# Two groups of spectral columns per turn in the middle stage of a Fourier MLP kernel, one 64-row stretch per turn, and the shared tile's relu on ScalarE

## The chip, the cores and the metric

The kernel runs on one core of a Trainium2 chip. The metric is the device time of one execution, in microseconds; lower is better. All data is fp32.

## The reference

An image batch `x` of shape (4, 128, 128, 768) goes through a Fourier layer: a real 2-D FFT over the two spatial axes, two small complex matrix layers in every spectral point, and the inverse FFT. The 768 channels fall into 8 blocks of 96, and each block has its own weights.

```
xf = rfft2(x, axes=(1, 2), norm='ortho')            # 65 columns kw, 128 rows kh
o1r = relu(xr @ w1[0] - xi @ w1[1] + b1[0]);  o1i = relu(xi @ w1[0] + xr @ w1[1] + b1[1])
o2r = o1r @ w2[0] - o1i @ w2[1] + b2[0];      o2i = o1i @ w2[0] + o1r @ w2[1] + b2[1]
o   = softshrink(o2, 0.01)                          # sign(v) * max(|v| - 0.01, 0)
out = irfft2(o, norm='ortho') + x
```

## The kernel before

The work is cut into 32 units (4 images times 8 channel blocks of 96). Each unit passes through six stages on TensorE: A (transform along one axis), B (first layer, on columns that are not yet transformed along the other axis; the two commute), C (transform along the other axis), D (second layer), E and F (inverse transforms). The next unit's stage A is mixed in after the present unit's inverse. An fp32 product appears in the trace as two MATMUL records, so a group's count is twice that of the code.

This case is about the middle of a unit, stages B, C and D, which the kernel calls `layers`. The 65 spectral columns are cut into `GROUPS`, 17 steps `s`: most have four columns (eight real and imaginary parts), step `REAL` = 2 holds columns 0 and 64, and the last has three. One step consists of:

- B whole, `stage_b_whole` (L778): four products with 128 contracted rows; B halved, `stage_b_halved` (L790): four products with 64 contracted rows, two row halves of the array at a time. A complex column needs 192 rows of input, so 128 + 64. VectorE then copies the result from PSUM to `mixed` (L655), and counts `b_copied`.
- C, `stage_c` (L807): six products with 128 rows, out of `mixed` into three tiles, of which the middle one is shared by the two halves. Their relu goes to `hidden` on ScalarE (L530, L533, `relu_done`), and the shared tile's relu to `middle` on VectorE (L668, `middle_done`).
- D outer, `stage_d_outer` (L822): four products with 128 rows; D middle, `stage_d_middle` (L832): four with 64 rows. They add to a bias that VectorE wrote to PSUM before (L678, the "seed"). ScalarE then computes the `excess` (L524), and VectorE the shrunk result (L663, `shrunk`), back into the spectrum.

ScalarE also gathers the columns of the next step into `whole` (L493, L494) and `halved` (L495, L496). `whole`, `halved`, `mixed`, `hidden` and `middle` have two buffers each, `excess` has one.

Every engine runs its own list in the order in which the code is written, and waits on semaphores. In turn `s` TensorE does B whole of step s, D of step s-2 (outer, middle), B halved of s, C of s-1. So each turn has one stretch of 64-row products (D middle, then B halved), and C works on a step whose copy to `mixed` was made one turn ago. Turns 0 and 1 have no D, and the last two steps' D have stretches of their own: 19 stretches in a unit. PSUM has eight banks: B takes 0 and 1 (step 1: 6 and 7), C takes 2 and 3, D takes 4 and 5 or 6 and 7, by the step's parity. `flip` (L839, L840), four records of 192 moving elements, symmetrises the `REAL` step's result.

Of the kernel before, what the change touches and what calls it, by code (L numbers as in the profile page):

```python
# [27 lines left out]
REAL = 2  # L28

# [130 lines left out]
def fourier_mlp(nc, x, w1, b1, w2, b2, dft, out):  # L160
    with ExitStack() as ctx:
# [26 lines left out]
        excess = sb("excess", [SIZE, BLOCK, 8])  # L188
        real_kw = sb("real_kw", [SIZE, BLOCK, 6])
# [32 lines left out]
        def banks_b(s):  # L222

            return 6 if s == 1 else 0

        def bank_b(s, k):

            if s == 1:
                return bank_d(s)[:, 2 * k:2 * k + 2]
            return bank(banks_b(s) + k // 2)[:, (k % 2) * 2 * BLOCK:(k % 2 + 1) * 2 * BLOCK]  # L230

        def both_b(s, i=None):
            if s == 1:

                return psum[:, banks_b(s):banks_b(s) + 2, 4 * i * SIZE // 2:4 * (i + 1) * SIZE // 2].rearrange(
                    "p y (r n) -> p y r n", r=2)[:, :, :, 0:BLOCK]
            return psum[:, banks_b(s):banks_b(s) + 2, 0:4 * BLOCK].rearrange("p y (i o) -> p i y o", i=2)


        bank_c = bank(2).rearrange("p (y i h) -> p y i h", y=2, i=2)  # L240
        middle_c = bank(3, SIZE, 2 * SIZE).rearrange("p (i h) -> p i h", i=2)

        def bank_d(s):

            pair = psum[:, 4 + 2 * (s % 2):6 + 2 * (s % 2), :].rearrange("p y n -> p (y n)")
            return pair.rearrange("p (q n) -> p q n", q=8)[:, :, 0:BLOCK]

# [7 lines left out]
        bank_flip = bank(0, SIZE, 2 * BLOCK).rearrange("p (k c) -> p k c", k=2)  # L255
# [36 lines left out]
        a_done, act_copied, dve_copied = sem("a_done"), sem("act_copied"), sem("dve_copied")  # L292
        b_done, b_copied = sem("b_done"), sem("b_copied")
# [90 lines left out]
        def _(sp):  # L384
# [10 lines left out]
            sp.dma_start(excess[:, :, :].rearrange("p a b -> p (a b)")[:, 0:2 * SIZE],  # L395
# [73 lines left out]
        def _(act):  # L469
            def gather(s):  # L470
                w, h, first = whole[s % 2], halved[s % 2], GROUPS[s][0]
                if s == REAL:
# [3 lines left out]
                    act.activation(h[0:HALF, :, 0], im[0:HALF, 0], ACT.Copy)  # L476
                    act.activation(h[HALF:SIZE, :, 0], im[0:HALF, 1], ACT.Copy).then_inc(halved_gathered, 1)
                    return
                j = 2 + 2 * first
                if s == 0:  # L480

                    act.activation(w[0:BLOCK, :, slice(*INNER)], first_parts(*INNER)[0:BLOCK, 0], ACT.Copy).then_inc(whole_gathered, 1)  # L482
                    return
                if GROUPS[s][3] is None:
# [3 lines left out]
                    act.activation(w[BLOCK:SIZE, 1, :, 0], U[HALF:BLOCK, :, j + 5], ACT.Copy).then_inc(whole_gathered, 1)  # L488
                    act.activation(h[0:HALF], U[0:HALF, :, j + 2:j + 4], ACT.Copy)
                    act.activation(h[HALF:SIZE, :, 0], U[0:HALF, :, j + 5], ACT.Copy).then_inc(halved_gathered, 1)  # L490
                    return
                parts = U[:, :, j:j + 8].rearrange("p s (y c r) -> p c y s r", y=2, c=2)
                act.activation(w[0:BLOCK], parts[0:BLOCK, 0], ACT.Copy)  # L493
                act.activation(w[BLOCK:SIZE], parts[HALF:BLOCK, 1], ACT.Copy).then_inc(whole_gathered, 1)  # L494
                act.activation(h[0:HALF], parts[0:HALF, 1, 0], ACT.Copy)  # L495
                act.activation(h[HALF:SIZE], parts[0:HALF, 1, 1], ACT.Copy).then_inc(halved_gathered, 1)  # L496

            def forward(n):
                for at in A_ACT:
                    act.wait_ge(a_done, n * NA + (at + 1))  # L500
                    src = bank_a(at).rearrange("p (s j) -> p s j", s=A_ROWS)
                    rows, third = evict_views(A_ORDER[at])
                    act.activation(rows, src[0:BLOCK], ACT.Copy)
                    act.activation(third, src[BLOCK:], ACT.Copy).then_inc(act_copied, 1)
            def layers(m, par, n):
# [4 lines left out]
                gather(0)  # L510
                act.wait_ge(w_loaded[par], (m + 1) * W_LOADS * 16)
                for s in range(NS + 2):
                    if s + 1 < NS:
                        if s >= 1:
                            act.wait_ge(b_done, n * NS + s)
                        gather(s + 1)

                    for stage in ("sums", "tiles") if s < NS else ("tiles", "sums"):
                        if stage == "sums" and s >= 2:
                            t = s - 2  # L520
                            act.wait_ge(d_done, n * NS + (t + 1))
                            if t >= 1:
                                act.wait_ge(shrunk, n * NS + t)
                            act.activation(excess[:, :, 0:rows_d(t)], parts_d(t), ACT.Relu,  # L524
                                           bias=over[:, 0:1]).then_inc(excess_done, 1)
                        if stage == "tiles" and 1 <= s <= NS:
                            t = s - 1
                            act.wait_ge(c_done, n * NS + (t + 1))
                            tiles = hidden[t % 2]
                            act.activation(tiles[:, 0, 0:pairs(t)], bank_c[:, 0, 0:pairs(t)], ACT.Relu,  # L530
                                           bias=b1t[par][:, 0:1]).then_inc(relu_done, 1)
                            k = pairs(t) if None not in GROUPS[t] else 1
                            act.activation(tiles[:, 1, 0:k], bank_c[:, 1, 0:k], ACT.Relu,  # L533
                                           bias=b1t[par][:, 2:3]).then_inc(relu_done, 1)
                act.wait_ge(flip_done, n + 1)
                act.activation(U[:, 0:BLOCK, SIZE + 2:].rearrange("p c k -> p k c"), bank_flip,
                               ACT.Copy).then_inc(flip_copied, 1)
            def inverse(n):
# [23 lines left out]
        def _(dve):  # L562
            dve.memset(over[:, :], -LAMBDA).then_inc(padding_set, 1)
            iw = excess[:, :, :].rearrange("p a b -> p (a b)")[:, 0:2 * SIZE].rearrange("p (a b) -> p a b", a=2)
# [52 lines left out]
            def forward(n):  # L617
# [26 lines left out]
                dve.tensor_copy(halved[0][HALF:SIZE, slice(*INNER)], parts[0:HALF, 1, 1]).then_inc(first_halved, 1)  # L644
            def layers(m, par, n, first, last):
                for s in range(NS + 2):
                    if s < NS:
                        k = pairs(s)
                        dve.wait_ge(b_done, n * NS + (s + 1))
                        if s == 1:  # L650
                            for i in range(2):
                                flat = mixed[s % 2][:, i].rearrange("p y (r o) -> p y r o", r=2)
# [277 lines left out]
```

## Time and profile before

| | |
|---|---|
| time, median of 3 runs | 5098.28 us (5097.17 to 5102.1) |
| span of the profiled execution | 5094.2 us |
| TensorE matmul busy | 4981.3 us, 98% |
| TensorE weight load busy | 4673.3 us, 92% |
| VectorE busy | 3816.7 us, 75% |
| ScalarE busy | 2996.3 us, 59% |
| GpSimd busy | 1436.3 us, 28% |
| mean granted TensorE clock | 0.993 |

The span runs from the first to the last instruction of one profiled execution. A matmul's record lasts longer than the time until the next one can start, since they are pipelined, so the busy share of TensorE says that it hardly ever stands still, and not that it works at its peak. What a stage costs is seen in the distances between the starts of its groups.

### The profile page before, as it was taken

Reading aid. Unit: us, or ns where it says so; the run is one execution under the profiler, and the core shown is the slowest. Engines: PE = TensorE matmul, PEld = TensorE weight load, DVE = VectorE, ACT = ScalarE, POOL = GpSimd, SP = SyncE. Lnnn points to the kernel's source line nnn. Section 1 sums busy time; section 2 is a strip of 40 time slices with the busy share of each in tenths; the row PEclk is TensorE's granted clock in tenths of the full one; section 3 lists DMA queues with packets and bytes.
Section 4 is the critical chain, followed back from the end, with each engine's and each line's share of the span. In section 5 each row is a group of like instructions: output and inputs, shape, how many; then the busy total and the mean of one; then the engine's idle time right before and its main releaser. Section 6 shows DMA issues by size and latency. Waiting matters only on the chain.

```text
span 5094.2 us, 113221 instructions
## 1 busy us (share of the span) xinstructions
PE 4981.3 (98%) x40000; PEld 4673.3 (92%) x40000; DVE 3816.7 (75%) x6159; ACT 2996.3 (59%) x5409; POOL 1436.3 (28%) x905
## 2 busy tenths in 40 slices
PE   6999999999999999999999999999999999999997
PEld 6999999999999999999999999999999999999996
DVE  5777777777777777777777777777777777777876
ACT  4555655556655566555566555665556655556653
POOL 3033223332123332233321333312333123332220
PEclk8999999999999999999999999999999999999998
DMA  5044423444323443234442344432344323444233
GB/s 114 12 94 105 98 59 69 91 105 105 68 57 87 105 105 87 56 81 94 105 105 52 70 90 105 106 70 62 79 105 106 86 61 78 92 105 105 61 73 72
DMA packets 1699712, 430.24 MB, mean 84 GB/s; under 512 B 1698848, under 2 KB 1698976, under 8 KB 1699104
## 3 DMA queue, kind: packets, MB, share of 16 engines
q1 hardware_dynamic: 1696768, 421.83, 37.5%
q8 instruction: 346, 5.67, 0.5%
q14 instruction: 262, 2.15, 0.1%
q10 hardware_dynamic: 2336, 0.59, 0.1%
HBM read 220.84 MB, written 201.33 MB: 83 GB/s over the span
## 4 chain that ended last, share of the span: by engine, by line
PE 96%; DVE 2%; issue 1%; SPq 1%; ACT 0%; DMA 0%; DVEq 0%; ACTq 0%
PE psum L807 15%; PE psum L778 14%; PE psum L822 14%; PE psum L760 13%; PE psum L849 13%; PE psum L832 9%; PE psum L790 7%; PE psum L859 3%; PE psum L860 3%; PE psum L861 3%; DVE mixed L655 1%; SPq L387 1%; DVE spectrum L628 0%; PE psum L840 0%; PE psum L839 0%
## 5 line engine op out<-in xcount | busy, mean ns | idle before, releaser
L655 DVE COPY mixed<-psum 128x768 f32<-128x768 f32 (+1 forms) x512 | 477.4, 932 | 700.0 <-PE psum L790 700.0
L541 ACT ACTIVATE sums_high<-psum 128x512 fp32r<-128x512 f32 x768 | 459.2, 599 | 731.3 <-PE psum L849 731.2
L807 PEld LDWEIGHTS psum<-mats,mixed 128*128 128x128 f32 x6272 | 744.0, 191 | 121.2 <-issue 113.1
L807 PE MATMUL psum<-mats,mixed 128*128 128x128 f32 x6272 | 841.8, 283 | 0.0
L778 PE MATMUL psum<-w_whole,whole 128*128 128x192 f32 x4160 | 782.3, 330 | 40.9 <-ACT whole L482 11.4
L822 PE MATMUL psum<-w2t,hidden 128*128 128x192 f32 x4160 | 771.7, 328 | 0.0
L849 PE MATMUL psum<-mats,spectrum 128*128 128x128 f32 x6144 | 743.7, 275 | 3.1 <-DVE spectrum L663 1.6
L760 PE MATMUL psum<-mats,x 128*128 128x128 f32 x6144 | 704.9, 277 | 33.6 <-DVE x L582 17.8
L760 PEld LDWEIGHTS psum<-mats,x 128*128 128x128 f32 x6144 | 696.0, 193 | 40.9 <-issue 23.0
L778 PEld LDWEIGHTS psum<-w_whole,whole 128*128 128x128 f32 x4160 | 673.3, 197 | 60.6 <-issue 33.7
L849 PEld LDWEIGHTS psum<-mats,spectrum 128*128 128x128 f32 x6144 | 714.5, 192 | 4.1 <-DVE sums_low L701 2.0
L701 DVE TENSOR_TENSOR sums_low<-psum,sums_high 128x512 fp32r<-128x512 f32 x768 | 530.4, 691 | 248.8 <-ACT sums_high L541 248.7
L822 PEld LDWEIGHTS psum<-w2t,hidden 128*128 128x128 f32 x4160 | 685.9, 190 | 13.4 <-issue 7.2
L524 ACT ACTIVATE excess<-psum,over 128x768 f32<-128x768 f32 (+1 forms) x544 | 481.8, 886 | 332.8 <-PE psum L832 329.9
L530 ACT ACTIVATE hidden<-psum,b1t 128x256 f32<-128x256 f32 (+1 forms) x544 | 254.6, 468 | 688.8 <-PE psum L807 688.8
L453 POOL TENSOR_TENSOR x<-x,half 128x3072 f32<-128x3072 f32 x32 | 169.8, 5307 | 1450.0 <-DVE halved L644 1450.0
L663 DVE SCALAR_TENSOR_TENSOR spectrum<-psum,excess 128x768 f32<-128x768 f32 (+1 forms) x512 | 480.8, 939 | 118.7 <-ACT excess L524 113.0
L678 DVE COPY psum<-b_rows 128x768 f32<-128x768 f32 (+1 forms) x544 | 504.0, 926 | 0.0
L436 POOL TENSOR_TENSOR x<-x 128x192 f32<-128x192 f32 x31 | 15.7, 505 | 1700.4 <-DMA x<-x 1700.4
L832 PE MATMUL psum<-w2t,middle 64*128 64x192 f32 x4160 | 490.3, 350 | 0.0
L859 PE MATMUL psum<-sums_high,iw_high 128*128 128x260 f32 (+1 forms) x1536 | 461.8, 301 | 0.0
L445 POOL TENSOR_TENSOR x<-x,doubled 128x640 f32<-128x640 f32 (+1 forms) x248 | 443.4, 1788 | 17.0
(76 smaller groups left out, 7800.7 us busy)
## 6 DMA issues: line engine op xcount, KB each, us to landing
x<-x SPq DMA_DIRECT2D x736, 192.0 KB, 2.9
out<-x SPq DMA_DIRECT2D x736, 192.0 KB, 2.5
x<-x SPq DMA_DIRECT2D x736, 64.0 KB, 2.6
out<-x SPq DMA_DIRECT2D x736, 64.0 KB, 2.2
x<-x SPq DMA_DIRECT2D x32, 144.0 KB, 2.7
out<-x SPq DMA_DIRECT2D x32, 144.0 KB, 2.3
w2t<-L_conv_w SPq DMA_DIRECT2D x124, 36.0 KB, 1.8
x<-x SPq DMA_DIRECT2D x64, 48.0 KB, 2.4
```

What stands on the lines that cost most here:

```text
L524: act.activation(excess[:, :, 0:rows_d(t)], parts_d(t), ACT.Relu, bias=over[:, 0:1]).then_inc(excess_done, 1)
L655: copied = dve.tensor_copy(mixed[s % 2][:, 0:k], both_b(s)[:, 0:k])
L663: dve.scalar_tensor_tensor(dst, parts_d(t), LAMBDA, excess[:, :, 0:rows], op0=ALU.add, op1=ALU.min).then_inc(shrunk, 1)
L678: dve.tensor_copy(bank_d(s).rearrange("p (k r) c -> p k r c", r=2)[:, 0:k], b2_rows[par][:, :, :].unsqueeze(1).broadcast_to([SIZE, k, 2, B ...
L701: dve.tensor_tensor(sums_low[:, q % RING], bank_e(q), sums_high[:, q % RING], ALU.subtract).then_inc(low_copied, 1)
L760: last = pe.matmul(bank_a(at)[:, i * SIZE:(i + 1) * SIZE], xs[par][:, j, :], mat(FW_EVEN if g[0] < NP else FW_ODD), start=i == 0, stop=Tru ...
L778: pe.matmul(bank_b(s, k), whole[s % 2][:, k // 2, :, k % 2], w1_whole[par][:, :, :].rearrange("p r o -> p (r o)"), start=k % 2 == 0, stop= ...
L807: last = pe.matmul(out[tile], flat[:, tile * SIZE:(tile + 1) * SIZE], mat(FH), start=True, stop=True)
L822: pe.matmul(sums_d(s, k), hidden[s % 2][:, k // 2, k % 2], w2_tile(par, slice(0, SIZE), 2 * (k // 2)), start=False, stop=False, skip_group ...
L832: last = pe.matmul(sums_d(s, i + 2 * y), middle[s % 2][rows, i], w2_tile(par, rows, 1), start=False, stop=True, skip_group_check=True)
L849: last = pe.matmul(bank_e(q)[:, :, i], U[:, q * CHUNK + i, 4:], mat(IH_FIRST if q * CHUNK < THIRD else IH), start=True, stop=True)
L859: pe.matmul(out, iw_high[:, j], high, start=True, stop=False)
```

## The change

`layers` takes two steps a turn (`STEPS`: nine turns, the last with one step). With a and b the two steps of a turn and p and q those of the turn before, TensorE does: B whole a, B whole b, D outer p, D outer q, D middle p, D middle q, B halved a, B halved b, C a, C b. The 64-row stretch holds the second layer's tiles first and the first layer's last. In the first turn each step has its own B whole and B halved. After the ninth turn come `flip` and D of step 16.

With it:

- B and C of one step share a pair of banks (`pair_bc`: 0 and 1 for even steps, 6 and 7 for odd ones), D takes 4 and 5 or 2 and 3. B whole of step s therefore waits for the relus of step s-2.
- C of a step follows in the same turn as its B halved.
- ScalarE takes over the relu of the shared tile (`rectify`: three ACTIVATE instead of two), and `excess` has two buffers. ScalarE's order in a turn: gather whole for both steps ahead, gather halved for the first of them, the excess of p and q, the relus of a and b, gather halved for the second step ahead.
- VectorE's order in a turn: copy a, copy b, shrink p, shrink q, seed a, seed b, then what belongs to neighbouring units.
- The `REAL` step's result is stored part by part (`real_kw` is [6, 96] a partition, and was [96, 6]), so `flip` reads runs of 96 adjacent elements where it read every sixth by distance.
- In stage A the row `MIDDLE` is transformed first in its group; some start flags of A and F differ. TensorE waits for step 15's shrink before the next unit's stage A.

The diff, cut to its core (`MIDDLE` row and flags left out):

```diff
+STEPS = [tuple(range(s, min(s + 2, NS))) for s in range(0, NS, 2)]
+NT = len(STEPS)
...
-        excess = sb("excess", [SIZE, BLOCK, 8])
-        real_kw = sb("real_kw", [SIZE, BLOCK, 6])
+        excess = [sb(f"excess{i}", [SIZE, BLOCK, 8]) for i in range(2)]
+        real_kw = sb("real_kw", [SIZE, 6, BLOCK])
...
+        def pair_bc(s):
+            return 6 if s % 2 else 0
...
+            def surplus(n, s):
+                act.wait_ge(d_done, n * NS + (s + 1))
+                if s >= 2:
+                    act.wait_ge(shrunk, n * NS + (s - 1))
...
+            def rectify(par, n, s):
+                act.wait_ge(c_done, n * NS + (s + 1))
+                tiles, k = hidden[s % 2], pairs(s)
+                act.activation(tiles[:, 0, 0:k], bank_c(s)[:, 0, 0:k], ACT.Relu, bias=b1t[par][:, 0:1]).then_inc(relu_done, 1)
+                act.activation(middle[s % 2][:, 0:k], middle_c(s)[:, 0:k], ACT.Relu, bias=b1t[par][:, 1:2]).then_inc(middle_done, 1)
+                k = k if None not in GROUPS[s] else 1
+                act.activation(tiles[:, 1, 0:k], bank_c(s)[:, 1, 0:k], ACT.Relu, bias=b1t[par][:, 2:3]).then_inc(relu_done, 1)
...
+                for t, step in enumerate(STEPS):
+                    ahead = STEPS[t + 1] if t + 1 < NT else ()
+                    for s in ahead:
+                        act.wait_ge(whole_read, n * NS + (s - 1))
+                        gather_whole(s)
+                    for s in ahead[:1]:
+                        act.wait_ge(b_done, n * NS + (s - 1))
+                        gather_halved(s)
+                    if t > 0:
+                        for s in STEPS[t - 1]:
+                            surplus(n, s)
+                    for s in step:
+                        rectify(par, n, s)
+                    for s in ahead[1:]:
+                        act.wait_ge(b_done, n * NS + (s - 1))
+                        gather_halved(s)
...
             def stage_b_whole(par, n, s):
...
-                    pe.wait_ge(b_copied, n * NS + (s if s > 2 else 1))
+                    pe.wait_ge(relu_done, n * (2 * NS) + 2 * (s - 1))
+                    pe.wait_ge(middle_done, n * NS + (s - 1))
                 pe.wait_ge(whole_gathered, n * NS + (s + 1))
...
             def stage_c(n, s):
                 pe.wait_ge(b_copied, n * NS + (s + 1))
...
-                if s >= 1:
-                    pe.wait_ge(relu_done, n * (2 * NS) + 2 * s)
-                    pe.wait_ge(middle_done, n * NS + s)
...
             def layers(par, n):
...
+                for t, step in enumerate(STEPS):
+                    before = STEPS[t - 1] if t > 0 else ()
+                    for s in step:
                         stage_b_whole(par, n, s)
+                        if t == 0:
+                            stage_b_halved(par, n, s)
+                    for s in before:
+                        stage_d_outer(par, n, s)
+                    for s in before:
+                        stage_d_middle(par, n, s)
+                    if t > 0:
+                        for s in step:
+                            stage_b_halved(par, n, s)
+                    for s in step:
+                        stage_c(n, s)
+                flip(n)
+                stage_d_outer(par, n, NS - 1)
+                stage_d_middle(par, n, NS - 1)
```

How TensorE's list stands before, from the middle of a unit: one turn and the start of the next. The names are those of the tiles; in brackets is what the instruction waits for, and a count is in products, not in records.

```order
L778 MATMUL psum<-w_whole,whole 128x192 [waits whole_gathered]
L778 MATMUL psum<-w_whole,whole 128x192 x3
...
L822 MATMUL psum<-w2t,hidden 128x2x96 [waits seeded,relu_done]
...
L832 MATMUL psum<-w2t,middle 128x2x96 [waits middle_done]
L832 MATMUL psum<-w2t,middle 128x2x96 x3
...
L790 MATMUL psum<-w_halved,halved 128x192 [waits halved_gathered]
L790 MATMUL psum<-w_halved,halved 128x192 x3
L807 MATMUL psum<-mats,mixed 128x128 [waits middle_done,relu_done,b_copied]
L807 MATMUL psum<-mats,mixed 128x128 x5
L775 REGISTER_ALU [waits b_copied]
L778 MATMUL psum<-w_whole,whole 128x192 [waits whole_gathered]
```

The same place in the changed kernel, from D middle of step q on:

```order
L863 MATMUL psum<-w2t,middle 128x2x96 [waits middle_done]
L863 MATMUL psum<-w2t,middle 128x2x96 x3
...
L827 MATMUL psum<-w_halved,halved 128x192 [waits halved_gathered]
L827 MATMUL psum<-w_halved,halved 128x192 x3
L838 MATMUL psum<-mats,mixed 128x128 [waits b_copied]
L838 MATMUL psum<-mats,mixed 128x128 x5
L838 MATMUL psum<-mats,mixed 128x128 [waits b_copied]
L838 MATMUL psum<-mats,mixed 128x128 x5
...
L811 REGISTER_ALU [waits middle_done,relu_done]
L814 MATMUL psum<-w_whole,whole 128x192 [waits whole_gathered]
L814 MATMUL psum<-w_whole,whole 128x192 x3
```

In the second list B halved of a (two rows like those of b) stands at the first line of dots. The two groups at L838 are C of a and of b. What moved: C of a step stood behind one whole turn after its B halved, and now only the other step's B halved lies between; and B whole, which waited for `b_copied`, now waits for relus.

ScalarE's list before, one turn:

```order
L493 ACTIVATE whole<-spectrum 96x512 [waits b_done]
L494 ACTIVATE whole<-spectrum 32x512
L495 ACTIVATE halved<-spectrum 64x256
L496 ACTIVATE halved<-spectrum 64x256
L524 ACTIVATE excess<-psum,over 128x768 [waits shrunk,d_done]
L530 ACTIVATE hidden<-psum,b1t 128x256 [waits c_done]
L533 ACTIVATE hidden<-psum,b1t 128x256
```

And in the changed kernel, from the first step's gather halved to the end of a turn:

```order
L507 ACTIVATE halved<-spectrum 64x256 [waits b_done]
L508 ACTIVATE halved<-spectrum 64x256
L525 ACTIVATE excess<-psum,over 128x768 [waits shrunk,d_done] x2
L531 ACTIVATE hidden<-psum,b1t 128x256 [waits c_done]
L532 ACTIVATE middle<-psum,b1t 128x256
L534 ACTIVATE hidden<-psum,b1t 128x256
L531 ACTIVATE hidden<-psum,b1t 128x256 [waits c_done]
L532 ACTIVATE middle<-psum,b1t 128x256
L534 ACTIVATE hidden<-psum,b1t 128x256
```

Three ACTIVATE now stand behind each C, and what runs ahead of the first of them begins with a wait for B halved (`b_done`); the excess row stands for both steps.

## Rows read from the trace of the kernel before

**Rows 1.** The page: span, busy times by engine, the chain that ended last.

```profile
span 5094.2 us, 113221 instructions
...
PE 4981.3 (98%) x40000; PEld 4673.3 (92%) x40000; DVE 3816.7 (75%) x6159; ACT 2996.3 (59%) x5409; POOL 1436.3 (28%) x905
...
PE 96%; DVE 2%; issue 1%; SPq 1%; ACT 0%; DMA 0%; DVEq 0%; ACTq 0%
```

**Rows 2.** The waits of TensorE: for what, us in total, times, longest.

```profile
PE psum L778 <- ACT whole L482: 11.4, 25, 0.6
...
PE psum L778 <- DVE mixed L655: 8.4, 32, 0.3
```

**Rows 3.** Timeline of TensorE, one unit's ends: start, us, engine, line, count.

```profile
2399.84 18.14 PE L760 MATMUL psum<-mats,x 128*128 128x128 f32 x161
...
2419.82 1.57 PE L778 MATMUL psum<-w_whole,whole 128*128 128x192 f32 x8 [0.43 <-ACT whole L482]
...
2515.14 2.05 PE L760 MATMUL psum<-mats,x 128*128 128x128 f32 x16
```

**Rows 4.** The same for another unit.

```profile
1637.96 1.58 PE L778 MATMUL psum<-w_whole,whole 128*128 128x192 f32 x8 [0.43 <-ACT whole L482]
...
1733.29 2.05 PE L760 MATMUL psum<-mats,x 128*128 128x128 f32 x16
```

**Rows 5.** Timeline of TensorE, one turn in the middle of a unit.

```profile
2441.00 1.47 PE L778 MATMUL psum<-w_whole,whole 128*128 128x192 f32 x8
2442.31 1.46 PE L822 MATMUL psum<-w2t,hidden 128*128 128x192 f32 x8
2443.70 0.92 PE L832 MATMUL psum<-w2t,middle 64*128 64x192 f32 x8
2444.46 0.82 PE L790 MATMUL psum<-w_halved,halved 64*128 64x192 f32 x8
2445.21 1.60 PE L807 MATMUL psum<-mats,mixed 128*128 128x128 f32 x12
2446.65 1.47 PE L778 MATMUL psum<-w_whole,whole 128*128 128x192 f32 x8
```

**Rows 6.** Timeline of all engines in that turn, rows of weight loads, ScalarE, VectorE.

```profile
2440.78 0.39 PE L807 MATMUL psum<-mats,mixed 128*128 128x128 f32 x2
...
2441.20 0.47 ACT L530 ACTIVATE hidden<-psum,b1t 128x256 f32<-128x256 f32 x1 [1.41 <-PE psum L807]
2441.22 0.47 DVE L668 TENSOR_SCALAR middle<-psum,b1t 128x256 f32<-128x256 f32 x1
2441.58 0.47 ACT L533 ACTIVATE hidden<-psum,b1t 128x256 f32<-128x256 f32 x1
...
2443.31 0.45 ACT L495 ACTIVATE halved<-spectrum 64x256 f32<-64x256 f32 x1
2443.70 0.63 PEld L832 LDWEIGHTS psum<-w2t,middle 64*128 64x128 f32 x8 [0.23 <-issue]
...
2443.77 0.44 ACT L496 ACTIVATE halved<-spectrum 64x256 f32<-64x256 f32 x1
...
2444.67 0.90 ACT L524 ACTIVATE excess<-psum,over 128x768 f32<-128x768 f32 x1 [0.47 <-PE psum L832]
2445.20 1.41 PEld L807 LDWEIGHTS psum<-mats,mixed 128*128 128x128 f32 x12 [0.22 <-issue]
...
2445.32 0.96 DVE L655 COPY mixed<-psum 128x768 f32<-128x768 f32 x1 [1.10 <-PE psum L790]
```

**Rows 7.** TensorE behind a copy of VectorE (step 3), from two timelines.

```profile
2435.03 0.94 PE L807 MATMUL psum<-mats,mixed 128*128 128x128 f32 x6
2435.15 0.96 DVE L655 COPY mixed<-psum 128x768 f32<-128x768 f32 x1 [1.34 <-PE psum L790]
...
2436.24 1.57 PE L778 MATMUL psum<-w_whole,whole 128*128 128x192 f32 x8 [0.27 <-DVE mixed L655]
```

**Rows 8.** TensorE behind a relu (step 0), timeline.

```profile
2425.99 0.82 PE L778 MATMUL psum<-w_whole,whole 128*128 128x192 f32 x4
2426.19 0.47 ACT L530 ACTIVATE hidden<-psum,b1t 128x256 f32<-128x256 f32 x1 [1.61 <-PE psum L807]
...
2426.71 0.62 PEld L822 LDWEIGHTS psum<-w2t,hidden 128*128 128x128 f32 x4 [0.20 <-ACT hidden L530]
```

**Rows 9.** Timeline of TensorE, `flip` and what follows it.

```profile
2508.41 0.84 PE L839 MATMUL psum<-real_kw,mats 128*128 128x192 f32 x2
2509.06 0.86 PE L840 MATMUL psum<-real_kw,mats 128*128 128x192 f32 x2
2509.74 1.29 PE L807 MATMUL psum<-mats,mixed 128*128 128x128 f32 x10
```

**Rows 10.** One line each: the relus of the shared tile and of the first tile.

```profile
L668 DVE TENSOR_SCALAR middle<-psum,b1t x544: 339/475/485, 78.1 to 5014.5; 128x256 f32<-128x256 f32 x172, 128x128 f32<-128x128 f32 x10
...
L530 ACT ACTIVATE hidden<-psum,b1t x544: 367/474/477, 78.1 to 5014.5; 128x256 f32<-128x256 f32 x172, 128x128 f32<-128x128 f32 x10
```

More of the change, by code:

```diff
@@ L469, in _, with gather_whole @@
         def _(act):
-            def gather(s):
-                w, h, first = whole[s % 2], halved[s % 2], GROUPS[s][0]
-                if s == REAL:
+            def gather_whole(s):
+                w, j = whole[s % 2], 2 + 2 * GROUPS[s][0]
+                if s == 0:
+                    act.activation(w[0:BLOCK, :, slice(*INNER)], first_parts(*INNER)[0:BLOCK, 0], ACT.Copy).then_inc(whole_gathered, 1)
+                elif s == REAL:
                     re, im = (U[:, :, j:j + 2].rearrange("p s k -> p k s") for j in (2, SIZE + 2))
@@ L509, in layers @@
                 act.wait_ge(dve_copied, (n + 1) * len(A_DVE))
-                gather(0)
+                gather_whole(0)
+                gather_whole(1)
+                gather_halved(1)
                 act.wait_ge(w_loaded[par], (m + 1) * W_LOADS * 16)
-                for s in range(NS + 2):
-                    if s + 1 < NS:
-                        if s >= 1:
[L515 to L534, printed above, removed]
@@ L563, in _ @@
             dve.memset(over[:, :], -LAMBDA).then_inc(padding_set, 1)
[L564 removed]
+            iw = excess[0][:, :, :].rearrange("p a b -> p (a b)")[:, 0:2 * SIZE].rearrange("p (a b) -> p a b", a=2)
             dve.wait_ge(iw_loaded, 16)
@@ new lines, in evict_b, with shrink @@
+            def evict_b(n, s):
+                k = pairs(s)
+                dve.wait_ge(b_done, n * NS + (s + 1))
+                dve.tensor_copy(mixed[s % 2][:, 0:k], both_b(s)[:, 0:k]).then_inc(b_copied, 1)
+            def shrink(n, s):
+                rows, j = rows_d(s), 2 + 2 * GROUPS[s][0]
+                dve.wait_ge(excess_done, n * NS + (s + 1))
+                if s == REAL:
+                    dve.scalar_tensor_tensor(real_kw[:, :, :], real_d(), LAMBDA, real_excess(), op0=ALU.add,
+                                             op1=ALU.min).then_inc(shrunk, 1)
+                else:
+                    dve.scalar_tensor_tensor(U[:, 0:BLOCK, j:j + rows], parts_d(s), LAMBDA, excess[s % 2][:, :, 0:rows], op0=ALU.add,
+                                             op1=ALU.min).then_inc(shrunk, 1)
@@ new lines, in seed @@
+            def seed(par, n, s):
+                k = rows_d(s) // 2
+                if s == 1:
+                    dve.wait_ge(f_late_added, n * LATE)
+                elif s >= 2:
+                    dve.wait_ge(shrunk, n * NS + (s - 1))
+                dve.tensor_copy(bank_d(s).rearrange("p (k r) c -> p k r c", r=2)[:, 0:k],
+                                b2_rows[par][:, :, :].unsqueeze(1).broadcast_to([SIZE, k, 2, BLOCK])).then_inc(seeded, 1)
+            def layers(m, par, n, first, last):
+                for t, step in enumerate(STEPS):
+                    for s in step:
+                        evict_b(n, s)
+                    for i in range(2):
+                        if t > 0:
+                            shrink(n, STEPS[t - 1][i])
+                        if t + 1 == NT and i < len(step):
+                            seed(par, n, step[i])
+                    if t + 1 < NT:
+                        for s in step:
+                            seed(par, n, s)
+                    for s in range(2 * t, 2 * t + 2):
+                        if 2 <= s < 2 + 2 * NP and not first:
+                            unfold_step(n - 1, 1 - par, s - 2)
+                        if 2 + 2 * NP <= s < 2 + 2 * NP + W_SIGNS and not last:
+                            prepare_step(m + par, 1 - par, s - 2 - 2 * NP)
+                shrink(n, NS - 1)
```

147 lines of the change are left out of this document (55 added, 92 removed).

## The prediction

> **What bounds the kernel now.** I read the page first: TensorE's matmuls cover 98% of the span and the chain that ended last is 96% TensorE, while VectorE and ScalarE are busy for 75% and 59% [rows 1]. So only TensorE's own list counts, and the question is what in it is not work. The waits answer little: B whole waits 11.4 us in all for a gather at the head of the units, and 32 times for VectorE's copy [rows 2]. The rest is in the distances between starts. One unit's B, C and D last from 2419.82 to 2515.14, that is 95.32 us, and in another unit from 1637.96 to 1733.29, 95.33 us [rows 3, 4]; 32 such stretches make 3050 us, 60% of the span, and the change touches nothing else that has a price.
>
> Inside such a stretch a turn lasts 5.65 us [rows 5]. What its work needs can be read off: B whole puts 8 records of 192 elements into 1.31 us, 0.1625 us each. A long run of records with 128 elements takes (18.14 - 0.28) / 160 = 0.1117 us each [rows 3]. In a 64-row group two records run side by side: the group of 8 lasts 0.82 us, of which the last record is 0.32 and two records' offset 0.01, so three distances take 0.49, again 0.1625 each [rows 5]. A turn has 16 records of B whole and D outer (2.60), 8 pairs of D middle and B halved (1.30) and 12 records of C (1.34): 5.24. The other **0.40 us** lies at the two ends of the 64-row stretch. From D outer to D middle are 1.39 us instead of 1.30, and to B halved 0.76 instead of 0.65; then 0.75 to C instead of 0.65, and C takes 1.44 instead of 1.34 [rows 5]. The weight loads, which otherwise run ahead, stand at just these two places for 0.23 and 0.22 us with nothing to wait for but the array [rows 6].
>
> **What it saves, for one unit.**
> - Stretches: 19 before, 11 after (two in the first turn, one in each of eight, one for step 16). 8 x 0.40 = 3.20 us.
> - `flip`: its 4 records take 2509.74 - 2508.41 = 1.33 us, against 4 x 0.1625 = 0.65 for the same length read from adjacent elements in B whole [rows 9, 5]. I take the nearest row, 0.65, so 0.68 saved; the bounds are 0 and 0.68.
> - Old waits that go: step 3's B whole would have come at 2435.03 + 0.10 + 6 x 0.1117 = 2435.80 and came at 2436.24, and its group took 1.57 instead of 1.47, as its first weights weren't there [rows 7, 5]: 0.54. Step 0's D outer came at 2426.71 instead of 2425.99 + 0.65, and as late with its weights: 0.17 [rows 8].
>
> Sum 4.59 us. The start flags and the row `MIDDLE` change no record's length or count: nothing. Seeds, shrinks and ScalarE's gathers are as many as before; what covers them is checked below.
>
> **What it adds: the wait of C.** C of step a needs VectorE's copy of B halved a. Before, a whole turn lay between. Call E the end of B halved a's last record. VectorE starts 0.04 after E and copies for 0.96 (2445.28, 2445.32) [rows 5, 6]; TensorE's next record starts 0.05 after the releaser where the wait is on the weight load itself (2426.66 to 2426.71) [rows 8], and 0.13 after it where a register instruction stands between (2436.11 to 2436.24) [rows 7]. C waits directly: it can start at E + 1.05. Without a wait it would start at E + 0.58: B halved b's last record starts 0.65 after that of a, C 0.25 behind (0.09 more than one distance), and a's last record lasts 0.32. So C stands for **0.47 us**; nothing covers it, since C b, B whole and D stand behind C a. This falls on turns 2 to 7 (6 x 0.47 = 2.82). In turn 1, step `REAL` copies half as much, 0.56 instead of 0.96: C waits 0.07 there, and C of step 3 waits behind the second copy 0.28 and loads its weights late, 0.10: 0.45. In the ninth turn step 16 is alone: C could start 0.07 before E and starts at E + 1.05, 1.12. Sum 4.39.
>
> **The wait of B whole.** B whole of the next step a needs the three relus of C a, since it writes to the same banks. After the start of C a's last record come 0.28 until it ends, 0.04 until ScalarE starts, two distances of 0.37 or 0.38 and the third ACTIVATE's 0.47, and 0.13 to TensorE: 1.66 us [rows 6, 7]. In that time TensorE has C b and the step to the next, 13 x 0.1117 = 1.45. B whole stands for 0.21 and loads its first weights late, 0.10: **0.31 us**. B whole of b comes 1.30 + 0.10 later and its relus end 1.34 later, so only its weight load is late: 0.04. Is ScalarE free when C a ends? C a's last record starts at E + 1.05 + 0.21 + 10 x 0.1117 = E + 2.38, its end reaches ScalarE at E + 2.70. Until then it has gather halved (0.46 + 0.44) from E + 0.04 and two `excess` (0.80 each, 0.90 less the 0.10 by which such rows overlap): E + 2.54. Just free. Turns 3 to 8: 6 x 0.31 + 5 x 0.04 = 2.06. At the head: B whole of step 2 0.31; step 3 comes after only 4 records and waits for the relus of step 1, 0.69; step 4 waits behind the two `excess`, since C of `REAL` is short, 0.49. Sum 3.55. D outer of step 16 now follows `flip` directly and needs the relu of step 16: 0.27.
>
> VectorE after two copies has two shrinks, two seeds (0.95 each) and at most two unfold steps (1.75 each), 9.3 us in a turn of 11.7; it is free again 2 us before the next copy, and the seeds are ready 1.3 us before D outer.
>
> **The sum.** -4.59 + 4.39 + 3.55 + 0.27 = **+3.62 us** a unit; a double turn goes from 11.29 to 11.70. 32 units: +116 us. The profiled execution's span is 5094.2, the median 4.1 above it, so 5098.3 + 116 = **5214 us**.
>
> What would raise a term: B whole now waits for two semaphores before the one on its weight load. If the second costs a further 0.10 at each of some 16 B wholes, that is +51 us (5265). What would lower it: the distances after a late weight load may be hidden when the wait is short, 0.10 at some 14 places, -45 us (5169).
>
> ScalarE and VectorE take 474 and 475 ns for the relu of 256 elements [rows 10], so the move itself shifts a price without raising it; only the chain behind C gets one link of 0.37 longer. The Trainium skill (ScalarE: Activation LUTs, Rules for kernel authors) says to use VectorE for relu, and gives under What ACT_TABLE_LOAD costs about 280 ns + 0.833 ns an element for an ACTIVATE with a bias pointer, with an overlap of 93 ns. By those figures, as an estimate, the three relus take 2 x 400 + 493 = 1293 ns where rows give 1.21 us, and each full wait of B whole is 0.08 longer, about +20 us in all (5234). The trace has the durations, so the sum goes by it.
>
> **The rivals.**
> - *ScalarE keeps up.* If three relus in a row took under 1.45 us from C a's last record, B whole wouldn't wait: -3.82 a unit, a gain of 0.2, 5092 us: no change. Against it: the distances 0.37 and 0.38 in the same turn [rows 6].
> - *Reading PSUM gets faster* (faster than before). Copies and relus read banks next to those that TensorE writes, and which banks these are changes. If that had slowed them and now ended, so that the copy took under 0.49 and the relus under 1.45, all waits vanish: -4.59 a unit, 4951 us; the kernel is faster than before once 3.6 of the 8.2 us of waits are gone. Against it: the copy has 0.96 at both rows seen, with TensorE in different groups [rows 6, 7].
> - *The second semaphore is dear*, as above: 5265 us.
> - *A stretch's 0.40 doesn't go with its number*, but with the groups in it. Then 3.20 a unit isn't saved: 5316 us. Against it: the weight load stands only at its two ends, and between D middle and B halved it doesn't [rows 6].
>
> **How the numbers follow.** Forecast 0.74; dear semaphore 0.12; ScalarE keeps up 0.07; faster PSUM 0.04; no saving 0.03. The forecast's own bounds are 5169 and 5265; distances read to 0.01 us, some twenty of them in a unit's sum, leave another 0.2 to 0.4 us a unit, about 10 us. The range is 5158 to 5272. A difference under 0.2% (10 us) can't be told from none: faster 0.06, same 0.06, slower 0.88.
>
> **What the profile after would show.** From the first B whole of a unit to the next stage A some 99 us instead of 95.3, and 11.7 us from turn to turn. Waits of C for VectorE's copy (`mixed`), 0.3 to 0.5 us each, some 8 a unit, and of B whole for ScalarE's `hidden`; weight loads that stand for the array 22 times a unit and not 38. `flip` at 0.65 us. ScalarE up by 544 x 0.47 = 256 us of work and VectorE down by as much [rows 10]. Wrong would be C starting within 0.6 us of E, or stretches that cost other than 0.40.

## The result and the profile after

The changed kernel takes **5207.17 us** (median of 4 runs, 5205.15 to 5208.21), the kernel before 5097.92 us in the same comparison: ratio 1.0211, 95% interval 1.0197 to 1.0226. It is 2.1% slower. The prediction was 5214 us, with a range of 5158 to 5272. The profiled execution's span grew from 5094.2 to 5205.7 us, by 111.5 us; 116 were forecast.

The page of the changed kernel, its busy times and the chain that ended last, beside [rows 1]:

```profile
span 5205.7 us, 113043 instructions
...
PE 4956.1 (95%) x40000; PEld 4696.4 (90%) x40000; DVE 3632.8 (70%) x5583; ACT 3181.8 (61%) x5953; POOL 1437.3 (28%) x905
...
PE 89%; DVE 5%; ACT 3%; issue 2%; SPq 1%; DMA 0%; DVEq 0%; ACTq 0%
```

TensorE's matmuls are busy for less time than before (4956 us against 4981, with the same 40000 records) in a longer span. VectorE has 5% of the chain and ScalarE 3%, where they had 2% and 0%: they have become links in it. The waits of TensorE show where, beside [rows 2]:

```profile
PE psum L838 <- DVE mixed L677: 112.3, 224, 1.1
PE psum L814 <- ACT hidden L534: 20.5, 64, 0.4
```

C (L838) waits 224 times for VectorE's copy, seven times in each of 32 units. This wait was not there before at all. B whole (L814) shows up for ScalarE's relus only 64 times, because the view counts only time in which no matmul record runs, and the last record before a short wait lasts into it; the starts tell the rest. The timeline of TensorE, one unit's head and one full double turn in its middle:

```profile
2473.43 1.58 PE L814 MATMUL psum<-w_whole,whole 128*128 128x192 f32 x8 [0.45 <-ACT whole L481]
...
2478.16 2.94 PE L838 MATMUL psum<-mats,mixed 128*128 128x128 f32 x24
2481.14 0.92 PE L814 MATMUL psum<-w_whole,whole 128*128 128x192 f32 x4
2482.48 1.57 PE L814 MATMUL psum<-w_whole,whole 128*128 128x192 f32 x8 [0.42 <-ACT hidden L534]
2483.89 2.76 PE L853 MATMUL psum<-w2t,hidden 128*128 128x192 f32 x16
...
2509.54 1.47 PE L827 MATMUL psum<-w_halved,halved 64*128 64x192 f32 x16
2511.42 2.94 PE L838 MATMUL psum<-mats,mixed 128*128 128x128 f32 x24 [0.41 <-DVE mixed L677]
2514.40 2.91 PE L814 MATMUL psum<-w_whole,whole 128*128 128x192 f32 x16
2517.14 2.76 PE L853 MATMUL psum<-w2t,hidden 128*128 128x192 f32 x16
2519.84 1.57 PE L863 MATMUL psum<-w2t,middle 64*128 64x192 f32 x16
2521.24 1.47 PE L827 MATMUL psum<-w_halved,halved 64*128 64x192 f32 x16
```

From one B halved to the next, 2509.54 to 2521.24, are 11.70 us for two steps; before it was twice 5.65 [rows 5]. B halved to C takes 1.88 us, of which eight pairs account for 1.30 and the exit of the stretch for 0.10: C stands for 0.48. C to B whole takes 2.98 instead of 0.10 + 24 x 0.1117 = 2.78: 0.20. B whole to D outer takes 2.74 instead of 2.60: the weights are late at two places, 0.10 in front of the first B whole's second record and 0.04 at the second B whole.

The same stretch with the other engines shows why:

```profile
2510.41 1.82 DVE L677 COPY mixed<-psum 128x768 f32<-128x768 f32 x2 [3.10 <-PE psum L827]
...
2511.31 1.69 ACT L525 ACTIVATE excess<-psum,over 128x768 f32<-128x768 f32 x2
2511.42 2.75 PEld L838 LDWEIGHTS psum<-mats,mixed 128*128 128x128 f32 x24 [0.70 <-DVE mixed L677]
...
2513.06 0.47 ACT L531 ACTIVATE hidden<-psum,b1t 128x256 f32<-128x256 f32 x1
2513.43 0.47 ACT L532 ACTIVATE middle<-psum,b1t 128x256 f32<-128x256 f32 x1
2513.79 0.48 ACT L534 ACTIVATE hidden<-psum,b1t 128x256 f32<-128x256 f32 x1
```

VectorE sat idle for 3.10 us before its copy, so it isn't too busy: it gets its input too late. The copy starts at 2510.41, 0.04 after B halved of a ends, and C's first weight load follows 1.01 us later. The third relu starts at 2513.79 and ends at 2514.27; the weight load of B whole comes 0.12 us behind. At the unit's end step 16 stands alone:

```profile
2566.36 0.81 PE L827 MATMUL psum<-w_halved,halved 64*128 64x192 f32 x6
2568.22 1.38 PE L838 MATMUL psum<-mats,mixed 128*128 128x128 f32 x10 [1.05 <-DVE mixed L677]
2569.44 0.49 PE L869 MATMUL psum<-real_kw,mats 128*128 128x192 f32 x2
2569.77 0.49 PE L870 MATMUL psum<-real_kw,mats 128*128 128x192 f32 x2
2570.17 1.24 PE L853 MATMUL psum<-w2t,hidden 128*128 128x192 f32 x6
...
2572.19 1.38 PE L795 MATMUL psum<-mats,x 128*128 128x128 f32 x10
```

From the first B whole to the next stage A, 2572.19 - 2473.43 = 98.76 us for a unit's B, C and D, against 95.32 [rows 3]. This is the median of the 32 units in both traces, and their sums differ by 109 of the 111.5 us, so the loss lies here. `flip` takes 0.33 us for two records where it took 0.65 [rows 9]. And the weight loads that stand for the array, from the waits of TensorE's loads in the changed kernel:

```profile
PEld psum L863 <- issue: 64.8, 288, 0.2
...
PEld psum L827 <- issue: 14.8, 64, 0.4
```

and in the kernel before:

```profile
PEld psum L832 <- issue: 122.4, 544, 0.2
...
PEld psum L790 <- issue: 14.6, 64, 0.4
```

Entries into a stretch went from 608 (19 a unit) to 352 (11 a unit), each with the same 0.22 to 0.23 us of standing weight loads. What the change was made of worked; the new waits were dearer. One more forecast of the profile was off: ScalarE was to go up by 256 us and VectorE down by as much, and they moved by 185.5 and 183.9. Busy time counts once what two overlapping records share, and relus of 0.47 us stand 0.37 apart; 544 x 0.37 would be 201, and some of the relus are shorter. The forecast of the time doesn't rest on it.

### The profile page after: what moved, and what is told of

It reads as the page before. It is cut to its first block, busy times and chain, and to the rows that moved or that the text cites. A ratio compares the mean times of both kernels' runs of the same rounds, so it can differ in the third digit from the quotient of the medians.

```text
span 5205.7 us, 113043 instructions
## 1 busy us (share of the span) xinstructions
PE 4956.1 (95%) x40000; PEld 4696.4 (90%) x40000; DVE 3632.8 (70%) x5583; ACT 3181.8 (61%) x5953; POOL 1437.3 (28%) x905
## 3 DMA queue, kind: packets, MB, share of 16 engines
q8 instruction: 345, 5.65, 0.5%
## 4 chain that ended last, share of the span: by engine, by line
PE 89%; DVE 5%; ACT 3%; issue 2%; SPq 1%; DMA 0%; DVEq 0%; ACTq 0%
PE psum L814 14%; PE psum L838 13%; PE psum L853 13%; PE psum L795 13%; PE psum L879 13%; PE psum L863 8%; PE psum L827 4%; DVE mixed L677 4%; PE psum L889 3%; PE psum L890 3%; PE psum L891 3%; ACT excess L525 1%; SPq L394 1%; DVE spectrum L656 0%; ACT middle L532 0%
## 5 line engine op out<-in xcount | busy, mean ns | idle before, releaser
L677 DVE COPY mixed<-psum 128x768 f32<-128x768 f32 (+1 forms) x544 | 490.4, 931 | 1087.9 <-PE psum L827 1085.0
L838 PEld LDWEIGHTS psum<-mats,mixed 128*128 128x128 f32 x6272 | 724.2, 192 | 203.4 <-DVE mixed L677 196.4
L838 PE MATMUL psum<-mats,mixed 128*128 128x128 f32 x6272 | 785.2, 280 | 116.3 <-DVE mixed L677 112.3
L814 PE MATMUL psum<-w_whole,whole 128*128 128x192 f32 x4160 | 782.4, 338 | 60.0 <-ACT hidden L534 20.5
L814 PEld LDWEIGHTS psum<-w_whole,whole 128*128 128x128 f32 x4160 | 673.1, 197 | 137.4 <-issue 93.8
L853 PE MATMUL psum<-w2t,hidden 128*128 128x192 f32 x4160 | 726.4, 327 | 0.0
L853 PEld LDWEIGHTS psum<-w2t,hidden 128*128 128x128 f32 x4160 | 682.1, 190 | 6.7 <-ACT hidden L531 6.6
L525 ACT ACTIVATE excess<-psum,over 128x768 f32<-128x768 f32 (+1 forms) x512 | 432.4, 889 | 154.2 <-PE psum L863 149.3
L687 DVE SCALAR_TENSOR_TENSOR spectrum<-psum,excess 128x768 f32<-128x768 f32 (+1 forms) x512 | 465.8, 941 | 84.0 <-ACT excess L525 80.5
L507 ACT ACTIVATE halved<-spectrum 64x256 f32<-64x256 f32 x448 | 194.6, 434 | 530.7 <-PE psum L827 529.9
L697 DVE COPY psum<-b_rows 128x768 f32<-128x768 f32 (+1 forms) x544 | 481.5, 928 | 1.1
L446 POOL TENSOR_TENSOR doubled<-x 128x640 f32<-128x640 f32 (+1 forms) x248 | 357.2, 1440 | 312.9 <-DMA x<-x 299.4
```

What stands on the lines that cost most here:

```text
L525: act.activation(excess[s % 2][:, :, 0:rows_d(s)], parts_d(s), ACT.Relu, bias=over[:, 0:1]).then_inc(excess_done, 1)
L677: dve.tensor_copy(mixed[s % 2][:, 0:k], both_b(s)[:, 0:k]).then_inc(b_copied, 1)
L687: dve.scalar_tensor_tensor(U[:, 0:BLOCK, j:j + rows], parts_d(s), LAMBDA, excess[s % 2][:, :, 0:rows], op0=ALU.add, op1=ALU.min).then_inc( ...
L697: dve.tensor_copy(bank_d(s).rearrange("p (k r) c -> p k r c", r=2)[:, 0:k], b2_rows[par][:, :, :].unsqueeze(1).broadcast_to([SIZE, k, 2, B ...
L814: last = pe.matmul(bank_b(s, k), whole[s % 2][:, k // 2, :, k % 2], w1_whole[par][:, :, :].rearrange("p r o -> p (r o)"), start=k % 2 == 0 ...
L838: last = pe.matmul(out[tile], flat[:, tile * SIZE:(tile + 1) * SIZE], mat(FH), start=True, stop=True)
```

## The experiments

The theory on record: eight stretches fewer save 0.40 us each; C's wait for the copy, and B whole's wait for a chain of three relus, cost more than that. Rivals: the wait of C is the array's own (a longer stretch takes longer to leave); B whole waits for something other than the third relu; a stretch's price belongs to its groups. The times below are medians of 4 runs (11 where said), the ratios are against the kernel before on the same chip.

**First layer's tiles first.** In the changed kernel:

```diff
                     for s in before:
                         stage_d_outer(par, n, s)
-                    for s in before:
-                        stage_d_middle(par, n, s)
                     if t > 0:
                         for s in step:
                             stage_b_halved(par, n, s)
+                    for s in before:
+                        stage_d_middle(par, n, s)
```

> The changed kernel with one edit: in the 64-row stretch the first layer's tiles (B halved of a and b) come first and the second layer's (D middle of p and q) last. My theory (C stands for VectorE's copy, 0.47 us in turns 2 to 7, 0.45 in turn 1, 1.12 in turn 8): the 1.3 us of D middle now lie over the copy, these waits of 4.4 us a unit vanish, the wait of B whole for relus stays. First B whole to next stage A 94.1 to 94.4 us (98.76 in the changed kernel), time about 5060 us, so below the kernel before. Rival (C starts late because a longer 64-row stretch takes longer to leave, or because the array is what it waits for): the order inside the stretch doesn't matter, 5207 us.

Measured: 5072.74 us, ratio 0.9943 (0.9926 to 0.9959), 134 us less than the changed kernel. Its timeline of all engines:

```profile
2454.29 1.58 PE L827 MATMUL psum<-w_halved,halved 64*128 64x192 f32 x16
...
2455.27 1.82 DVE L677 COPY mixed<-psum 128x768 f32<-128x768 f32 x2 [1.99 <-PE psum L827]
2455.70 1.47 PE L863 MATMUL psum<-w2t,middle 64*128 64x192 f32 x16
...
2457.10 1.72 PE L838 MATMUL psum<-mats,mixed 128*128 128x128 f32 x13
```

The copy now has D middle over it (2455.70 to 2457.00), and C follows D middle in 1.40 us, eight pairs and the exit: no wait. The same groups in the other order take 4.2 us less a unit (94.53 against 98.76; 4.4 were expected). The time is 13 us above the 5060 expected: in every unit D outer of step 16 now stands idle some 0.3 for its seed, `PE psum L853 <- DVE psum L697` with 8.8 us in 32 waits, and starts 0.76 behind the second pair of `flip` instead of 0.40, 12 us in all. So C waited for the copy, and not for the array. This order alone makes the change worth 0.6% instead of costing 2.1%.

**Shared tile's relu back on VectorE.** In the changed kernel the ACTIVATE to `middle` goes, and VectorE does:

```diff
                     for i in range(2):
                         if t > 0:
                             shrink(n, STEPS[t - 1][i])
+                        if t + 1 < NT:
+                            rectify_middle(par, n, step[i])
...
+                rectify_middle(par, n, NS - 1)
                 shrink(n, NS - 1)
```

> The changed kernel with one edit: the relu of the shared tile goes back to VectorE, put before the second step's shrink and before the seeds. My theory (B whole waits for a chain of three relus on ScalarE, 1.66 us against 1.45): the chain is 0.37 shorter, B whole no longer waits in turns 3 to 8 and less in turns 1 and 2, about 3.1 us a unit; the waits of C stay. Some 95.7 us from first B whole to stage A, time about 5109 us. Rival (it is the two semaphores and the register instruction, or the banks, and not the third relu): 5207 us. Rival 2 (VectorE's relu now comes late behind the shrink): 5207 us or more, with B whole waiting for VectorE.

Measured: 5153.68 us, ratio 1.0104 (1.0087 to 1.0121), 53 us less than the changed kernel where 98 were expected. TensorE's timeline, a double turn (the edit moved the lines: L847 is C, L823 B whole, L862 D outer here):

```profile
2483.27 2.94 PE L847 MATMUL psum<-mats,mixed 128*128 128x128 f32 x24 [0.41 <-DVE mixed L676]
2486.05 2.77 PE L823 MATMUL psum<-w_whole,whole 128*128 128x192 f32 x16
2488.66 2.76 PE L862 MATMUL psum<-w2t,hidden 128*128 128x192 f32 x16
```

C to B whole takes 2.78 and B whole to D outer 2.61: neither wait nor late weights are left in the full turns, as the theory says; the turn is 11.37. C's wait stays. What is missing of the expected gain, 1.4 us a unit, lies mostly at the ends. A row from the ninth turn reads

```profile
2533.21 1.05 PE L862 MATMUL psum<-w2t,hidden 128*128 128x192 f32 x5 [0.55 <-DVE psum L696]
```

With two relus of 0.48 us in its list, VectorE seeds 0.8 us later (4.40 us behind the start of its copies, where it was 3.58); a short B whole (step 16, six records) no longer covers that, and D outer of step 14 waits. From the start of that B whole to D outer are 1.70 us, and were 1.09. This I hadn't worked out. The rest is missing at the head of the unit: there the edit saves 0.59 us (B whole of step 3 still waits for the relus of step 1, 0.52 where it was 0.69), and about 1.0 was expected.

**Both edits.**

> Both edits of the two other runs in the changed kernel: first layer's tiles first, shared tile's relu on VectorE. My theory: the two waits are independent and their gains add, 98.76 - 4.4 - 3.1 = 91.3 us a unit, about 4969 us, 2.5% below the kernel before: what is left is the saving of eight stretches and of flip. Rival (the two waits hide each other, so that removing one exposes another): between 5040 and 5109 us.

Measured: 5016.77 us, ratio 0.9841 (0.9825 to 0.9857), 190 us less than the changed kernel; the two edits alone gave 134 and 53, together 187. They add, so the waits are independent. It is 48 us above the 4969 expected. The seed's wait of the run before is missing again, and B whole of step 3, which costs 0.6 us with its late weights; and in 25 of the 32 units D outer of step 16 waits for its seed too, as with the first edit alone. A double turn in its timeline:

```profile
2562.80 2.77 PE L823 MATMUL psum<-w_whole,whole 128*128 128x192 f32 x16
...
2570.91 2.94 PE L847 MATMUL psum<-mats,mixed 128*128 128x128 f32 x24
2573.69 0.98 PE L823 MATMUL psum<-w_whole,whole 128*128 128x192 f32 x5
```

2562.80 to 2573.69 are 10.89 us. The work of two steps (2 x 5.24) and one stretch (0.40) make 10.88: nothing else is left in it.

**Two stretches a turn, in the kernel before.** This tests the price of a stretch itself.

```diff
+                    if s < NS:
+                        stage_b_halved(par, n, s)
                     if s >= 2:
                         stage_d_outer(par, n, s - 2)
                         stage_d_middle(par, n, s - 2)
-                    if s < NS:
-                        stage_b_halved(par, n, s)
```

> The kernel before with one edit: B halved comes right behind B whole, ahead of D, so that it no longer shares its 64-row stretch with D middle. 15 turns of a unit then have two stretches instead of one; the work is the same and every copy comes earlier. My theory (each stretch costs 0.40 us at its ends): 15 x 0.40 = 6.0 us more a unit, less 0.5 to 0.7 for the waits of steps 3 and 0 that go: +5.3 us, about 5268 us. Rival (the 0.40 belongs to the groups and not to the number of stretches): 5075 to 5098 us.

Measured: 5265.04 us, ratio 1.0324 (1.0307 to 1.0341); 5268 was expected. One turn, TensorE and then its weight loads:

```profile
2525.75 1.47 PE L778 MATMUL psum<-w_whole,whole 128*128 128x192 f32 x8
2527.15 0.93 PE L790 MATMUL psum<-w_halved,halved 64*128 64x192 f32 x8
2528.01 1.57 PE L822 MATMUL psum<-w2t,hidden 128*128 128x192 f32 x8
2529.50 0.92 PE L832 MATMUL psum<-w2t,middle 64*128 64x192 f32 x8
2530.36 1.60 PE L807 MATMUL psum<-mats,mixed 128*128 128x128 f32 x12
2531.80 0.50 PE L778 MATMUL psum<-w_whole,whole 128*128 128x192 f32 x2
```

```profile
2527.15 0.64 PEld L790 LDWEIGHTS psum<-w_halved,halved 64*128 64x128 f32 x8 [0.22 <-issue]
2528.01 1.27 PEld L822 LDWEIGHTS psum<-w2t,hidden 128*128 128x128 f32 x8 [0.22 <-issue]
2529.50 0.63 PEld L832 LDWEIGHTS psum<-w2t,middle 64*128 64x128 f32 x8 [0.23 <-issue]
2530.35 1.41 PEld L807 LDWEIGHTS psum<-mats,mixed 128*128 128x128 f32 x12 [0.23 <-DVE mixed L655]
```

The turn lasts 6.05 us against 5.65, with as many records: 0.40 us for one stretch more, and the weight loads stand at four places instead of two. The price goes with the number of stretches.

**The smaller parts, each alone in the kernel before** (11 runs each). First `flip`'s layout:

```diff
-        real_kw = sb("real_kw", [SIZE, BLOCK, 6])
+        real_kw = sb("real_kw", [SIZE, 6, BLOCK])
...
-                pe.matmul(bank_flip, mat(FLIP_RE), real_kw[:, :, 0::4].rearrange("p c k -> p k c"), start=True, stop=False)
+                pe.matmul(bank_flip, mat(FLIP_RE), real_kw[:, 0::4], start=True, stop=False)
```

> The kernel before with one edit: the result of the step REAL is stored part by part, so that flip's four records read runs of 96 adjacent elements. My theory: each goes from 0.33 to 0.16 us and C of the last step starts 0.68 us earlier: 32 x 0.68 = 22 us less, about 5076 us. Rival (the next relu or copy is then waited for, or VectorE's scattered write costs more): 5090 to 5098 us.

Measured: 5093.64 us, ratio 0.9990 (0.9981 to 0.9999): 4.6 us less, and not 22. The rival holds:

```profile
2505.91 0.49 PE L839 MATMUL psum<-real_kw,mats 128*128 128x192 f32 x2
2506.24 0.49 PE L840 MATMUL psum<-real_kw,mats 128*128 128x192 f32 x2
2507.06 1.13 PE L807 MATMUL psum<-mats,mixed 128*128 128x128 f32 x8 [0.34 <-ACT hidden L533]
```

`flip` is 0.66 us shorter, as forecast, but there it covered the relus for which C of step 16 waits. C starts 0.82 after `flip`'s second pair of records instead of 0.33, and most of the gain is gone.

Then the row `MIDDLE` and the start flags alone (the hunks of the change on stage A and F):

> The kernel before with the remaining parts of the change alone: in stage A the row MIDDLE is transformed first in its group, and the start flags of A and F are those of the changed kernel. My theory: no record's length or place changes, 5098 us within 0.2%. Rival: flags or order cost something, 5110 us or more.

Measured: 5098.27 us, ratio 1.0000 (0.9991 to 1.0009). They do nothing to the time.

Then the shared tile's relu on ScalarE, in the kernel before:

```diff
+                            act.activation(middle[t % 2][:, 0:pairs(t)], middle_c[:, 0:pairs(t)], ACT.Relu,
+                                           bias=b1t[par][:, 1:2]).then_inc(middle_done, 1)
...
-                            dve.tensor_scalar(middle[t % 2][:, 0:pairs(t)], middle_c[:, 0:pairs(t)], b1t[par][:, 1:2], 0.0,
-                                              ALU.add, ALU.max).then_inc(middle_done, 1)
```

> The kernel before with one edit: the shared tile's relu on ScalarE, between the two others. My theory (the move costs only where B whole stands right behind the next C): here a whole turn lies between C and the next C, which waits for the relus, ScalarE has 1.8 us to spare in a turn of 5.65, so no change, 5098 us within 0.2%. Rival (a third relu on ScalarE costs in any order): 5150 us or more.

Measured: 5105.26 us, ratio 1.0015 (1.0006 to 1.0024). It is under 0.2%, but the interval excludes no change: 7 us, 0.2 a unit. The starts in its trace put it at two places, D middle of step 0 (0.07 us later) and C of step 16 (0.12 later, and 0.08 for its late weights), which again follow a relu directly; all full turns have 5.64. Taking the relu back to VectorE saves 53 us in the changed kernel, where VectorE's late seeds take part of the gain away; so the same move costs some seven times as much there.

**The places that still waited, mended.** On top of both edits:

```diff
+                    if t == 0:
+                        seed(par, n, 0)
...
-                        if t + 1 == NT and i < len(step):
+                        if i < len(step) and t + 2 >= NT:
                             seed(par, n, step[i])
-                    if t + 1 < NT:
+                    if t == 0:
+                        seed(par, n, 1)
+                    elif t + 2 < NT:
                         for s in step:
                             seed(par, n, s)
...
+                        if t == 1:
+                            stage_d_outer(par, n, s - 2)
-                    for s in before:
+                    for s in before if t > 1 else ():
                         stage_d_outer(par, n, s)
```

> The kernel with both edits (first layer's tiles first, shared tile's relu on VectorE), 5017 us, with the two places mended at which its trace still waits: in the first turn and the last but one VectorE seeds earlier, between the relus, and in the second turn D outer of step 0 stands between the B wholes of steps 2 and 3. My theory: the waits of D outer of step 14 for its seed (0.6 to 0.7 us) and of B whole of step 3 for the relus of step 1 (0.6) go, 92.7 - 1.2 = 91.5 us a unit, about 4978 us. Rival (the wait moves on to the next relu or seed): 5000 to 5017 us.

Measured: **4983.74 us**, ratio 0.9772 (0.9757 to 0.9787), the fastest of all. From its timeline:

```profile
2529.11 0.82 PE L827 MATMUL psum<-w_whole,whole 128*128 128x192 f32 x4
2529.77 1.46 PE L866 MATMUL psum<-w2t,hidden 128*128 128x192 f32 x8
2531.07 1.46 PE L827 MATMUL psum<-w_whole,whole 128*128 128x192 f32 x8
```

L827 is B whole here and L866 D outer. D outer of step 0 stands 0.66 behind four records of B whole, and B whole of step 3 directly behind it. A unit's B, C and D take 91.55 us in the median; 91.5 was expected, and 4978 us in all. The idle time of D outer before seeds fell from 24.5 us (57 waits, 25 of them at step 16, which the expectation hadn't named) to 4.4 (16 waits, all at step 16).

## Why the prediction was right

By its own terms, for one unit, from the rows above and the same timelines in turns 1 and 2:

| term | forecast | measured |
|---|---|---|
| `flip`, saved | 0.68 | 1.33 - 2 x 0.33 = 0.67 |
| one stretch | 0.40 | 0.40 (turn of 6.05 against 5.65 with one more) |
| C waits, turns 2 to 7 | 0.47 | 0.48 |
| C waits, turn 8 | 1.12 | 1.86 - 0.65 - 0.10 = 1.11 |
| B whole, turns 3 to 8, with late weights | 0.31 + 0.04 | 0.20 + 0.10 + 0.04 = 0.34 |
| C waits, turn 1, with late weights | 0.45 | 0.07 + 0.28 + 0.10 = 0.45 |
| B wholes of steps 2 and 3 | 1.00 | 0.20 + 0.69 + 0.11 = 1.00 |
| B whole of step 4, with late weights | 0.49 | 0.40 + 0.10 = 0.50 |
| D outer of step 16 | 0.27 | 0.07 + 0.10 = 0.17 |
| double turn | 11.70 | 11.70 |
| sum | +3.62 | 98.76 - 95.32 = +3.44 |

The forecast was high by 7 us, and these 0.18 a unit make 6 of them. 0.10 is D outer of step 16. No other term is off by more than 0.01 at one place; the rest of the 0.18 is spread over some forty distances read to 0.01 us, and no term can be named for it. Both waits are shown to be what they were said to be: in the full turns C's goes when D middle lies over the copy, B whole's when ScalarE has one relu less, each without the other, and the other distances stay within 0.02 us. Of the rivals, "ScalarE keeps up" and "reading PSUM gets faster" fell by the profile after: the copies last 0.96 and the relus stand 0.36 to 0.37 apart, as before. "The second semaphore is dear" fell too: behind the third relu's end the weight load comes after 0.12 us, as behind one semaphore (0.12 to 0.13) [rows 7]. "The price doesn't go with the number of stretches" fell by the run with two a turn.

Where my working was thin: eight records in 1.31 us are 0.164 each, and I took 0.1625; groups of 16 take 2.61 in the later runs, 0.163 each, so only 0.01 us a turn hangs on it. The saving of `flip` was put at 0.68 by its records' length. Its records came out so, but alone in the kernel before the layout gives 0.14 a unit, since a relu is then waited for. In the changed kernel the term stood beside the 0.27 for D outer of step 16, which is the same cover seen from the other side, so the sum came out right; the 0.27 itself was 0.10 too high. How much of it the layout gives in the changed kernel I did not run. And the expectations of later runs (5109, 4969) missed that VectorE's seeds come late once it does more in a turn, or once C stops waiting in the ninth turn; all three runs with one or both edits came out above what was expected.

## What to carry to other kernels

Merging stretches of 64-row products pays 0.40 us for each one fewer, but the same merge moves producer and consumer closer: before merging, write down for every copy and relu what TensorE does between its source and its use, and compare with length plus handoff (here 1.05 us for a copy of 768 elements, counted from the end of TensorE's record, and 1.65 for three relus, counted from the start of C's last record). Where two orders inside the merged stretch are free, put first what somebody else must still work on. Here this choice alone decided between 2.1% slower and 0.6% faster, and with the relus shared between two engines, and the ends mended, the same idea gives 2.3%. A group's shortening is only worth what no one waits for behind it.

## What the runs showed of the hardware

- The price of a stretch of 64-row products was the same 0.40 us with 4, 8 and 16 pairs in it (turns of 6.05, 5.65 and 10.89 us), and whether it stood before C or before D outer. It falls in four parts of about 0.10: before the stretch's first record, within its first group, before the first 128-row record behind it, and within that group. Swapping the groups inside the stretch changed its length by no more than 0.02 us.
- A wait costs more than its own length: the first group behind it takes 0.10 us longer, since its weights weren't loaded ahead. That holds at 0.07 us of waiting (D outer of step 0 before [rows 8]) as at 0.44 (step 3 before [rows 7]), so a very short wait is dear for its size. Behind a stretch the wait costs no more than itself: C of two steps takes 2.78 us with a wait of 0.48 in front (relu back on VectorE) and without one (both edits), since those first weights are late in either case.
- A moving operand of 192 elements read at a distance of six fp32 elements takes 0.33 us a record, and 0.16 read from adjacent ones. The Trainium skill (SBUF — State Buffer, Door 1: The DMA port swizzle, where it speaks of cachelines) says that an access which crosses to a new line of 16 bytes pays, without a figure; this trace agrees, with a factor of two; that it is the line which costs, and not something else in the distance of 24 bytes, no run here shows.
